# A two-layer graph network on one core: the second placing product behind chunk 21, the key spread behind hh, static scatters in twos, and ho's last table quarters by column halves

## The reference

```python
# layer 0: N = 64 + 192 nodes; the first 128 edges are hh, the next 640 oo, the rest (7296) ho
feat  = concat([x[src], x[dst]], axis=1)                  # per edge, 2048 wide
e_hh, e_oo, e_ho = relu(feat[part] @ W_part + b_part)     # W_part 2048 x 1024, three of them
logit = (e_f @ W_a + b_a)[:, 0]
alpha = softmax of logit over the edges that share a target
z     = segment_sum(alpha[:, None] * x[src], dst)         # 256 x 1024
out0  = relu(concat([x, z]) @ W_hn or W_on + bias)        # first 64 nodes W_hn, the others W_on
x     = layernorm(x + out0)
# layer 1: h = x @ W; e = exp(-leaky_relu(al[src] + ar[dst])); h' = segment sums of e * h[dst] / rowsum
x     = layernorm(x + elu(h'))
```

## Time and profile before

| what | us |
|---|---|
| median of 3 timed runs (lowest, highest) | 395.45 (393.61, 395.59) |
| the profiled execution | 393.18 |
| its span in the trace | 391.1 |
| PE busy | 330.0 (84%) |
| DVE busy | 301.7 (77%) |
| ACT busy | 190.6 (49%) |
| POOL busy | 139.2 (36%) |

### The profile page before, as it was taken

One profiled execution on the slowest core, in us unless ns is written; L12 is line 12 of the kernel. 1 busy time (PEld: TensorE's weight loads), 2 busy tenths in 40 slices (PEclk: granted clock), 3 DMA queues, 4 the chain that ended last, 5 costly groups with the idle time before them and its releaser, 6 DMA issues.

```text
span 391.1 us, 4666 instructions
## 1 busy us (share of the span) xinstructions
PE 330.0 (84%) x1434; PEld 253.7 (65%) x1434; DVE 301.7 (77%) x398; ACT 190.6 (49%) x287; POOL 139.2 (36%) x202
## 2 busy tenths in 40 slices
PE   1999999999977996999999999854899970899470
PEld 1778878676435773888888887633788850688220
DVE  1799999907899775999999999888476889535545
ACT  3744583220044167777777774532366681232243
POOL 3300050541107100499899776642023323007000
PEclk9999999999989997899999999995999995599786
DMA  7997798799998570001103000460639880000002
GB/s 236 412 406 271 262 346 270 296 243 303 348 410 302 178 268 4 2 2 55 54 0 95 18 1 2 112 210 2 222 106 347 301 313 0 0 2 0 1 0 107
DMA packets 17639, 63.63 MB, mean 163 GB/s; under 512 B 2234, under 2 KB 2236, under 8 KB 17360
## 3 DMA queue, kind: packets, MB, share of 16 engines
q1 hardware_dynamic: 13520, 50.34, 35.4%
q0 software_dynamic: 2096, 8.74, 7.8%
q10 hardware_dynamic: 2000, 4.26, 3.4%
HBM read 60.16 MB, written 3.16 MB: 162 GB/s over the span
## 4 chain that ended last, share of the span: by engine, by line
PE 62%; DVE 27%; ACT 4%; issue 4%; DMA 2%; SPq 0%; DVEq 0%; ACTq 0%
PE ps L1221 20%; PE ps L1063 11%; PE ps L1085 8%; DVE W_lo L666 5%; PE ps L1252 5%; PE ps L1260 4%; PE ps L1228 3%; PE ps L1111 3%; PE ps L1283 2%; PE ps L1315 2%; DMA x_nat<-in_x_dram 2%; ACT W_hi L431 1%; DVE A_tab L851 1%; DVE tile_val L687 1%; DVE small L953 1%
## 5 line engine op out<-in xcount | busy, mean ns | idle before, releaser
L431 ACT CAST W_hi<-W_raw 128x1024 fp32r<-128x1024 f32 x72 | 73.1, 1049 | 63.2 <-DMA W_raw<-in_L_gnn_W_ho_dram 19.5
L666 DVE TENSOR_TENSOR W_lo<-W_raw,W_hi 128x1024 fp32r<-128x1024 f32 x56 | 74.4, 1354 | 26.0 <-ACT W_hi L431 23.2
L901 DVE SCALAR_TENSOR_TENSOR ps<-ps,wa_bc 128x1024 f32<-128x1024 f32 x74 | 87.6, 1272 | 4.0 <-PE ps L1221 4.0
L364 POOL TENSOR_TENSOR W_lo<-W_raw,W_hi 128x1024 fp32r<-128x1024 f32 x16 | 39.5, 2475 | 82.1 <-ACT W_hi L431 82.1
L1221 PE MATMUL ps<-A_tab,oh 128*128 x148 | 54.6, 450 | 0.0
L390 POOL TENSOR_SCALAR sc_r<-irow,keys 128x64 f32<-128x64 f32 x74 | 33.0, 446 | 46.0 <-PE ps L1228 45.8
L1063 PE MATMUL ps<-W_hi,xT_hi 128*128 128x512 f32 x112 | 46.4, 414 | 2.2 <-DVE W_lo L666 2.2
L1221 PE MATMUL ps<-B_tab,oh 128*128 x148 | 47.6, 404 | 0.0
L1063 PE MATMUL ps<-W_lo,xT_hi 128*128 128x512 f32 x112 | 44.4, 396 | 0.0
L545 ACT ACTIVATE sc_l<-sc_l,keys 128x64 f32<-128x64 f32 x74 | 24.9, 343 | 23.2 <-DVE ps L901 17.0
L1063 PE MATMUL ps<-W_hi,xT_lo 128*128 128x512 f32 x112 | 35.0, 394 | 0.0
(11 more groups left out here) (223 smaller groups left out, 545.8 us busy)
## 6 DMA issues: line engine op xcount, KB each, us to landing
W_raw<-in_L_gnn_W_oo_dram SPq DMA_DIRECT2D x8, 1024.0 KB, 9.7
W_raw<-in_L_gnn_W_ho_dram SPq DMA_DIRECT2D x8, 1024.0 KB, 8.4
W_raw<-in_L_gnn_W_hh_dram SPq DMA_DIRECT2D x8, 1024.0 KB, 11.3
W_raw<-in_L_gnn_W_hn_dram SPq DMA_DIRECT2D x8, 1024.0 KB, 4.9
W_raw<-in_L_gnn_W_on_dram SPq DMA_DIRECT2D x8, 1024.0 KB, 4.9
W_raw<-in_L_gnn_W_dram SPq DMA_DIRECT2D x4, 1024.0 KB, 5.2
key_rows<-key_rows_scratch POOLq DMA_DIRECT2D x1, 2304.0 KB, 12.2
table_scratch<-tabs ACTq DMA_DIRECT2D x2, 1024.0 KB, 6.4
```

What stands on the lines that cost most here:

```text
L364: ga.tensor_tensor(W_lo[:, ring(n), :], W_raw[:, n // 2 % NS, n % 2, :], W_hi[:, ring(n), :].bitcast(F32), ALU.subtract).then_inc(lo_pool, 1)
L431: sa.copy(W_hi[:, ring(n), :], W_raw[:, n // 2 % NS, n % 2, :]).then_inc(hi_made, 1)
L666: v.tensor_tensor(W_lo[:, ring(n), :], W_raw[:, n // 2 % NS, n % 2, :], W_hi[:, ring(n), :].bitcast(F32), ALU.subtract).then_inc(lo_made, 1)
L901: v.scalar_tensor_tensor(acc, acc, 0.0, wa_bc[:], ALU.max, ALU.mult, accum_out=keys[:, t, 2:3]).then_inc(reduced, 1)
```

## The change

- PE: `perm(1)` goes behind chunk 21, ahead of hh 22, 23; the transposing of the keys behind hh 22, 23, the first count behind it, the second count behind ho 24, 25. Scatters stand in twos behind chunks 40, 41 and 42. The last four chunks of ho are multiplied by a new function, `last_of_hoB`: m = 0 as before, then m = 1 in two passes, columns 0 to 511 of all four chunks, then 512 to 1023. The wait for `hoB_lo` moves from ahead of the two bank openings to ahead of the first gather.
- DVE: `positions_of(1)` ahead of `low(24)`; `low(28)`, `low(29)` behind `key_u8`; `static_shares(1)` behind the first two static operands; operands 3 and 4 in a row; B's quarters 2 and 3 by halves.
- ACT: B's quarters 2 and 3 by column halves; `high(48)` to `high(50)` no longer between B's quarters, `high(51)` no longer ahead of the loop, but all four in the gather loop at j = 3, 9, 15 and 21.
- POOL: the spread of the other 72 tiles of keys waits until hh is done.

```diff
@@ -264,7 +264,7 @@
             return sum(split(m) and by_pool(m) == pool for m in range(n + 1))
 
 
-        PE_STAGES = ["xT0", "xT1", "totals", "x_rowsT", "perm0", "perm1", "keysT", "hoB_0", "PT", "zT0", "zT1", "q1",
+        PE_STAGES = ["xT0", "xT1", "totals", "x_rowsT", "perm0", "perm1", "keysT", "hoB_0", "hoB_1", "PT", "zT0", "zT1", "q1",
                      "x1T0", "x1T1", "h_0", "albc", "hp0", "hp1"]
         ACT_STAGES = ["xT0", "xT1", "hh_x", "ooB_out", "C_hh", "C_oo", "L_oo", "L_hh", "counts", "soft0", "soft1", "zT0", "both0", "zT1",
                       "both1", "q0_low", "q1_low", "sd0", "x1_0", "sd1", "x1T0", "x1T1", "h1_0", "h1_1", "lrelu",
@@ -395,10 +395,11 @@
             pool.dma_start(key_dram.rearrange("k t m -> t k m"), key_u8[:]).then_inc(keys_out, 16)
             pool.wait_ge(keys_out, 16)
             for a, b in ((0, 2), (2, NT)):
+                if a:
+                    pool.wait_ge(chunk_used, END["hh"])
                 pool.dma_start(key_rows[:, :, a * P:b * P],
                                key_dram[:, a:b, :].rearrange("k t m -> k (t m)").partition_broadcast(P)) \
                                    .then_inc(keys_back if a else first_keys_back, 16)
-            pool.wait_ge(chunk_used, END["hh"])
             for q in range(2):
                 for i, part in enumerate((xT_hi, xT_lo) if q == 0 else (xT_lo, xT_hi)):
                     ga.tensor_copy(x_both[:, :, q, i, :], part[:, :, q * Q:(q + 1) * Q]).then_inc(both_made, 1)
@@ -499,11 +500,12 @@
             act.wait_ge(counted, 2)
             take(S_cnt, 1, 3)
 
-            def table_high(tab, acc, a, b):
+            def table_high(tab, acc, a, b, f=0, width=D):
 
                 for q in range(a, b):
                     r = (q % 2) * Q
-                    sa.copy(tab[0:Q, q, :], acc[r:r + Q, (q // 2) * D:(q // 2 + 1) * D]).then_inc(quarter_hi, 1)
+                    sa.copy(tab[0:Q, q, f:f + width], acc[r:r + Q, (q // 2) * D + f:(q // 2) * D + f + width]) \
+                        .then_inc(quarter_hi, 1)
 
             act.wait_ge(dve_step, dve_at("hoA_b"))
             act.wait_ge(tabs_out[0], 16)
@@ -522,10 +524,10 @@
                    .then_inc(biases_in, 16)
             act.wait_ge(pe_step, pe_at("hoB_0"))
             table_high(B_tab, G1, 0, 2)
-            for n in range(END["hoB"], END["hoB"] + NB - 1):
-                high(n)
+            act.wait_ge(pe_step, pe_at("hoB_1"))
+            table_high(B_tab, G1, 2, 4, 0, D // 2)
             act.wait_ge(chunk_used, END["hoB"])
-            table_high(B_tab, G1, 2, 4)
+            table_high(B_tab, G1, 2, 4, D // 2, D // 2)
 
 
             def distance(j):
@@ -550,11 +552,12 @@
             onehot(0)
             act.wait_ge(keys_back, 16)
             distance(1)
-            high(END["hoB"] + NB - 1)
             for j in range(1, NT // 2):
                 onehot(j)
                 if j + 1 < NT // 2:
                     distance(j + 1)
+                if j % 6 == 3 and j // 6 < NB:
+                    high(END["hoB"] + j // 6)
                 if j >= 2:
                     scale_ends(2 * j - 4)
                     scale_ends(2 * j - 3)
@@ -777,8 +780,8 @@
             dve.wait_ge(pe_step, pe_at("perm0"))
             tile_values(1, 0)
             tile_values(1, 1)
+            positions_of(1)
             low(24)
-            positions_of(1)
             low(25)
 
 
@@ -843,26 +846,25 @@
                     link(v.tensor_tensor(acc[:, h * D:(h + 1) * D], acc[:, h * D:(h + 1) * D], bias_bc[:, k, :],
                                          ALU.add))
 
-            def low_quarter(tab, acc, before, a, b):
-
-                for q in range(a, b):
+            def low_quarter(tab, acc, before, a, b, f=0, width=D):
+
+                for i, q in enumerate(range(a, b)):
                     r = (q % 2) * Q
-                    dve.wait_ge(quarter_hi, before + q + 1)
-                    link(v.tensor_tensor(tab[Q:P, q, :], acc[r:r + Q, (q // 2) * D:(q // 2 + 1) * D],
-                                         tab[0:Q, q, :].bitcast(F32), ALU.subtract))
+                    dve.wait_ge(quarter_hi, before + i + 1)
+                    link(v.tensor_tensor(tab[Q:P, q, f:f + width], acc[r:r + Q, (q // 2) * D + f:(q // 2) * D + f + width],
+                                         tab[0:Q, q, f:f + width].bitcast(F32), ALU.subtract))
 
             dve.wait_ge(pe_step, pe_at("perm1"))
             link(v.tensor_copy(key_col[:].rearrange("p k t -> p (k t)"), bank(2)[:, 0:2 * NT]))
             link(v.tensor_copy(keys[:, :, 0:2], key_col[:].rearrange("p k t -> p t k")))
             stage("keys")
-            low(28)
-            low(29)
             dve.wait_ge(pe_step, pe_at("keysT"))
             link(v.tensor_copy(key_u8[:].rearrange("t k m -> t (k m)"), bank(3)[0:NT, 0:2 * P]))
             stage("key_u8")
-            for kind, count in ((0, "C_hh"), (1, "C_oo")):
-                dve.wait_ge(act_step, act_at(count))
-                static_shares(kind)
+            low(28)
+            low(29)
+            dve.wait_ge(act_step, act_at("C_hh"))
+            static_shares(0)
             dve.wait_ge(consts_in, 32)
             for t in range(1, JO + 1):
                 oo_logit(t)
@@ -875,23 +877,25 @@
             dve.wait_ge(st_oh_made, 2)
             static_operands(1, 0)
             static_operands(2, 1)
+            dve.wait_ge(act_step, act_at("C_oo"))
+            static_shares(1)
             lows(END["hh"], END["hh"] + 2)
             hh_logit()
             split_logits(0, 1)
             low(END["hh"] + 2)
             static_operands(3, 2)
+            static_operands(4, 3)
             low(END["hh"] + 3)
-            static_operands(4, 3)
-            low(END["hh"] + NB)
             static_operands(5, 4)
-            low(END["hh"] + NB + 1)
             static_operands(0, JO)
-            lows(END["hh"] + NB + 2, END["hoB"])
+            lows(END["hh"] + NB, END["hoB"])
             for kind, sums in ((1, "L_oo"), (0, "L_hh")):
                 dve.wait_ge(act_step, act_at(sums))
                 static_means(kind)
             link(v.tensor_tensor(top_static[:], S_log[:, 0, :, :], S_log[:, 1, :, :], ALU.max))
-            low_quarter(B_tab, G1, 4, 0, 4)
+            low_quarter(B_tab, G1, 4, 0, 2)
+            low_quarter(B_tab, G1, 6, 2, 4, 0, D // 2)
+            low_quarter(B_tab, G1, 8, 2, 4, D // 2, D // 2)
             stage("hoB_lo")
 
 
@@ -1090,6 +1094,22 @@
                     if m == 0 and first_block:
                         stage(ins, first_block)
 
+            def last_of_hoB():
+
+                for m, columns in ((0, (0, 512)), (1, (0,)), (1, (512,))):
+                    for n in range(END["hh"] + NB, END["hoB"]):
+                        W1, W0 = split_chunk(n)
+                        c = n - END["hh"]
+                        for part, Ws in ((xT_hi, (W1, W0)), (xT_lo, (W1,))):
+                            for f in columns:
+                                for W in Ws:
+                                    ins = mm(G1[:, m * D + f:m * D + f + 512], part[:, c, m * P:(m + 1) * P],
+                                             W[:, f:f + 512], start=False, stop=(c == KC - 1 and part is xT_lo))
+                        if columns == (512,):
+                            ins.then_inc(chunk_used, 1)
+                    if 0 in columns:
+                        stage(ins, f"hoB_{m}")
+
             def open_bank(b):
 
                 mm(bank(b), zero_b[0:1, 0:P], zero_b[0:1, :], start=True, stop=False, skip_group_check=True)
@@ -1170,19 +1190,19 @@
             perm(0)
             hh_dense(18, 20)
             hoA_dense(20, 22)
+            perm(1)
             hh_dense(22, 24)
-            hoA_dense(24, 26)
-            perm(1)
-            hh_dense(26, 28)
             pe.wait_ge(dve_step, dve_at("keys"))
             for k in range(2):
                 ins = nc.tensor.transpose(bank(3)[0:NT, k * P:(k + 1) * P], key_col[:, k, :], ident[:])
             stage(ins, "keysT")
             pe.wait_ge(st_oh_made, 2)
             count_static(0, [0], 2)
-            hoA_dense(28, 30)
+            hoA_dense(24, 26)
             pe.wait_ge(dve_step, dve_at("key_u8"))
             count_static(1, range(1, 1 + JO), 3)
+            hh_dense(26, 28)
+            hoA_dense(28, 30)
             hh_dense(30, END["hh"])
             pe.wait_ge(dve_step, dve_at("hoA_lo"))
             hoB = (G1, END["hh"], END["hoB"])
@@ -1192,14 +1212,13 @@
             scatter_static(2, 1)
             x_dense(END["hh"] + 1, END["hh"] + 2, *hoB)
             scatter_static(3, 2)
+            scatter_static(4, 3)
             x_dense(END["hh"] + 2, END["hh"] + 3, *hoB)
-            scatter_static(4, 3)
-            x_dense(END["hh"] + 3, END["hh"] + NB, *hoB)
             scatter_static(5, 4)
             scatter_static(0, JO)
-            block_by_block(END["hh"] + NB, G1, END["hh"], None, "hoB_0")
```

(5 more changed lines are left out.)

## The result

The changed kernel takes **383.46 us** (median of 4 runs, 382.76 to 384.90) against 395.44 for the kernel before (393.61 to 395.59): ratio 0.9719, 95% interval 0.9697 to 0.9741. Forecast were 386.2 and a range of 383.2 to 390.6. Its profiled execution took 383.35, span 381.3; the one before had 393.18 and 391.1. So the profiles differ by 9.8 us and the medians by 12.0.

What follows compares the result with a forecast made beforehand. PE was taken to bound the kernel (84% busy, 62% of the chain), DVE next (77%, 27%). Terms -5.9 - 0.3 - 2.1 - 1.0 = -9.3, put on the median 395.45, gave 386.2 us; range 383.2 to 390.6.

Steps and rivals of the forecast that it cites:

- Placing product, keys, DVE's chain: On PE and DVE before hoB: key_col at 79.3, bias after ho chunk 29 at 98.6, low(40) at 114.3; DVE's idleness goes.
- Spread behind hh: Keys spread after hh: its 40 matmuls end at 115.8, not 119.7, and hoB starts there: -5.9 us (0 to -6).
- Price of the late spread: Key transfer beside later weights: keys landed by 129, needed at 144; pair 46, 47 lands at about 124; no stall.
- rival 2: After hh, the keys starve weight pair 46, 47, which lands at 134: +3.0 us, 389.2; chance 8%.
- hoB: PE's hoB stretch with scatters two to a chunk: 26.5 us for 26.80, -0.3 (0 to -0.5; +1 if an operand is late).
- Halves: ho's last quarters by column halves: first gather 2.65 us after the last matmul, not 4.77: -2.1 (-0.8 to -2.5).
- Casts in the loop: ACT's casts high(48) to high(51) in the gather loop: cost 0, bounds 0 and 4.2 us.
- Clock at the first gathers: At the gather loop's start, 2.1 us hang on PE's clock; half taken, -1.0 us (0 to -2.1).
- From the profile to the median: Profiled execution, 393.18, lies 2.3 below the timed median, 395.45; the difference of -9.3 is put on the median: 386.2.
- Rivals 1 to 5: hh or low(40) waits, 391.1, 9%; keys starve weights, 389.2, 8%; casts show, 390.4, 6%; casts starve PE, 398.8, 5%; unchanged, 3%.

Runs made afterwards that it cites:

- the tail's experiment: The kernel before with only the scatters in twos, B's quarters by halves, the moved hoB_lo wait and casts in the gather loop: 391.45 us, ratio 0.9922.

## Why the prediction was right, step by step

The measured 383.46 lies 0.3 us above the foot of the range and below the 384 to 388.5 that the forecast called its own. The mechanism came out; the sizes agree less well than the totals do. From the start of hoB to the fourth reduction the parts forecast as -5.9, -0.3, -2.1 and -1.0 measured -5.8, -1.0, -2.0 and -1.85: -10.6 in place of -9.3. The clock behind the loop then took 0.8 back, so that the profiles differ by 9.8, near the sum. That nearness is partly luck.

- **Placing product, keys, DVE's chain.** Right to a few tenths: key_col 79.28 (forecast 79.3), bias 98.77 (98.7), low(40) from 113.28 (113.1). Undoing the placing product's place costs 5.9, and hoB then starts 4.2 us later.
- **Spread behind hh.** Right: 17.33 us for hh and hoB at 115.8. I had read the 5.9 as 3.9 of hh and 2.0 of DVE. The runs show that the parts can't be taken apart like that: the spread alone gives 0.0, since DVE's chain was as late, and DVE's part alone (the early spread back) starts hoB at 117.86, 3.8 earlier than before. How long PE waits for hh varies too: 2.02 in the profile of before, 0.61 in the tail's experiment with the same spread.
- **Price of the late spread.** The outcome was right, the working only in part. The flight was 14.0 us where I had 12.2, landed at 130, needed at 144; pair 46, 47 took 6.0 and landed at 121.9, where I had 124 from half each. The Trainium skill ("DMA: Bandwidth & Descriptors", "Queues, rings and completion order") states that each DMA engine goes round its queues a packet at a time. The trace agrees, but half of the packets isn't half of the bytes. From 125 to 128 us the two queues moved 79 packets each, and the keys' (q0, POOL's queue) were 9.2 KB against the weights' 4.1 (q1, SP's):

```profile
q0 software_dynamic: 79, 0.73, 63.0%
q1 hardware_dynamic: 79, 0.32, 30.8%
```

  That is packets, MB, share of the 16 engines. Beside the keys, weights get less than a third of the bytes. Pair 46, 47 was spared since the keys, issued at 116.1, moved nothing before 120 us, and it landed two later. No run shows what sets that delay, so how far rival 2 was off is open.
- **hoB.** The term was too small: -0.3 forecast, and 25.8 us were measured for 26.8, so -1.0. About 0.2 of it is how the start is read (behind idleness before, at hh's end now). Most of the rest are two short stops of PE in the kernel before: 0.2 us ahead of the second scatters, at 128.76, and 0.3 ahead of chunk 46, whose low part DVE starts at 138.70, behind ACT's copies of the sums. The second one comes back when the scatters do.

```profile
138.70 2.36 DVE L666 TENSOR_TENSOR W_lo<-W_raw,W_hi 128x1024 fp32r<-128x1024 f32 x2 [4.16 <-ACT W_hi L431]
...
139.98 0.50 PE L1085 MATMUL ps<-W_hi,xT_hi 128*128 128x512 f32 x1
```

- **Halves.** Right: 2.8 us between the last matmul and the first gather, forecast 2.65; the two pieces took 1.18 on ACT and 1.41 on DVE, as the 128x512 rows said.
- **Casts in the loop.** Cost nothing there, as forecast (85.99 us of loop for 85.98), but my account of them as an edit apart was wrong: undone they cost 3.2.
- **Clock at the first gathers.** Either answer is right in some executions; taking half was fair. The stake was too large: 2.1 us forecast, and 1.2 between the two profiled executions of the changed kernel.
- **From the profile to the median.** Here lie 2.2 of the 2.7 us of error; the other 0.5 is -9.8 for -9.3. I set the sum against the median as if the profiled execution of before stood 2.3 under it by rule. The one after stands 0.1 under its own. In 35 further runs of the kernel before, 393.57 to 397.00, none was as short as 393.18: it was a lucky one. What made it short is open, since its mean granted clock, 0.930, is that of runs that took 393.75 to 395.69.

Rivals 1 to 5 did not come about.

## What to carry to other kernels

Where two waits stand close together before a stage, find each one's own chain. Removing the one that ends earlier gives nothing (0.0 us here); removing the later one gives what lies between them; only both together give the whole. An edit that looks free (a cast moved out of the way, scatters in twos) can be what lets its neighbour pay. And take the profiled execution's place in the spread of the runs before turning a sum into a time.

## What the runs showed of the hardware that I had not expected

- **The spread of the runs goes with the granted clock, but not wholly.** On one chip the kernel before took 394.15 to 395.13 at a mean granted clock of 0.934 or 0.935 and 397.00 at 0.922; the changed one 382.71 to 383.20 at 0.941 and 384.66 at 0.929. At 0.930 alone the kernel before took 393.75 to 395.69.
- **The same idle stretch of PE, 2.2 us, gives either clock.** Before the first gather: full for the changed kernel (0.73) and with the scatters back (0.72), half in its repetition and with the early spread (1.22 each), half in the tail alone (1.12). With the shares early and with the placing product back it was full at first (0.73 and 0.72) and fell within the first tiles; the shares' median was no worse for it. After 3.29 and 4.41 us it was half both times, after 0.26 and 1.13 full.
- **Matmuls that nobody uses go with a held clock.** In the gap before the loop they were worth 1.1 us, in the stretches behind it 0.9670 - 0.9626 = 0.0044 of the time, 1.7 us; both lie within overlapping intervals, with the clock's rows behind them (1.00 from 230 to 320 us, for 0.89 without them).
- **The write of 18.5 KB of keys to DRAM took 14.4 us**, and 7.3 in the profile of before. It stands in POOL's queue behind the last gathered rows, which landed at 96.8 (before 97.2); the write landed at 98.2 (before 99.8). So issuing it 8.8 us earlier brought the keys back only 1.6 us earlier. That it waits for its own queue rather than for the weights fits these times; no run takes the two apart.
